# A fifth weight tile in the last group, 48 of 64 output groups turned while units run, and the first four weight slots freed one after another

## The chip, the cores and the metric

The kernel runs on all 8 cores of one Trainium2 chip. Each core takes 2048 of the 16,384 tokens and computes its whole result; the cores exchange nothing. The metric is the device time of the slowest core in microseconds (us). The two dies hold cores 0 to 3 and 4 to 7.

## The reference, cut to what matters

```python
# x: 4 x 4096 tokens of 4096 features
wb  = weight blocks (32 x 32), zeroed where the mask's block sums to 0
x1  = layernorm(x + x @ wb.T + bias)                    # layer 1
p   = softmax(x1 @ Wr.T); top 2 of 8 experts, renormed  # router
h   = einsum('ti,eri->ter', x1, A)                      # low rank, 8 x 16
lora = einsum('ter,te,eor->to', h, w, Bm) * 2
out = layernorm(x1 + x1 @ Wb.T + bias + lora)           # layer 2
```

Both layer norms run over the 4096 features of a token and have no gain or offset.

## The kernel before, in words

**Layout.** Activations lie transposed: features on the 128 partitions, tokens along the free axis. A core's 2048 tokens are four chunks (`tc` 0 to 3) of 512, its 4096 features 32 row tiles (`KT` = 32). `X` holds all of it in bf16. A weight tile (`n`, 32 for each layer) is 128 output features by 4096 inputs, 1 MB in bf16, cast by the DMA from 2 MB of f32; it lies in one of four slots `wt[0..3]` (tile number modulo 4).

**Units.** One unit is one weight tile by one chunk: 32 matmuls of 128x512 into one bank, and in layer 2 a 33rd for the low-rank part (`lora`, L484). `make_units` writes the order of all 260 units by hand, and every engine's program walks the same list, so `no` (1 to 260) is at once the unit's number and the value that semaphores `s_unit`, `s_evict`, `s_s1`, `s_s2` reach with it. Phase 0 is layer 1 (128 units), phase 1 layer 2 for chunks 0 and 1 (64 units), phase 2 layer 2 for chunks 2 and 3. VectorE evicts each unit (L660, L664: add the bias and the residual), ScalarE squares it (L928), VectorE adds both to the running sums `S1` and `S2` (L675, L682).

**The head.** The first 16 units (`HEAD`) take tiles 0 to 3 together, a chunk at a time: for each of eight pieces of X (four row tiles, one DMA of 1 MB f32 that becomes 512 KB, L305) all four tiles do four matmuls (L533 to L550). So units 13 to 16 end within a piece of each other. Tile 4 may be loaded into slot 0 once unit 13 is done (`LAST_OF_TILE`, L296). Phase 0's tiles need more: GpSimd loads the tile's mask in two halves into `ovA` (L290), VectorE sums its blocks (`sum_mask`, L620) and multiplies the weights (`clear_weights`, L635), which sets `s_wm`; TensorE waits for it. In the order of VectorE's program the sum of mask 4 comes after the eviction of unit 12, and the clearing of tile 4 after that of unit 14. All loads of masks, weights and X go through GpSimd's one queue, in program order. SyncE issues five small constants at the very start (L353 to L357), then the transposed residuals of phase 0 (`xres`, in `ovB`, L380).

**The tail.** Outputs of chunks 0 and 1 leave in the transposed layout through `ostg` (in `ovA`) and the host turns them; those 64 stores are over long before the end (the last is issued at 1735.5 us). Chunks 2 and 3 are turned on the core. The last four tiles (28 to 31, `GRP` = 4) run first for all of chunk 2, then for the first 256 tokens of chunk 3 (`FIRST_HALF`), then for its second 256 (`SECOND_HALF`), with 256-column matmuls. Sums per token come from `part_sums` in three parts (1024 tokens' first 512, next 256, last 256), each followed by `part_moments` on VectorE and `part_deviation` on ScalarE. There are 64 groups (128 tokens by 512 features): a `turn` is four matmuls against the identity (L528) into one of three side banks, `finish` scales the bank into an f32 stage in a dead part of `X` (L797 on VectorE for odd groups, L896 on ScalarE for even ones), and SyncE stores 256 KB (L413). `PART_AT` and `TURN_AT` say at which unit and after which matmul of it a part or a turn is issued. Groups 0 to 31 (chunk 2) are turned in units 254 to 260, up to five a unit; groups 32 to 63 after the last unit, when the four `pm` banks are free too (`tall`). A turn waits for the finish of the group three (then seven) before it, which has its bank.

Of the kernel before, what the change touches and what calls it, by code (L numbers as in the profile page):

```python
# [18 lines left out]
KT = D // 128  # L19
# [9 lines left out]
NW = 4  # L29
WT = KT + 1  # L30
# [3 lines left out]
NSQ = 2  # L34
NO = 4
GRP = 4


def make_units():

    u = [(0, n, tc) for tc in range(4) for n in range(GRP)]
    u += [(0, n, tc) for n in range(GRP, KT - GRP) for tc in range(4)]
    u += [(0, n, tc) for tc in (0, 1) for n in range(KT - GRP, KT)]
    u += [(0, n, tc) for n in range(KT - GRP, KT) for tc in (2, 3)]
    u += [(1, n, tc) for tc in (0, 1) for n in range(GRP)]
    u += [(1, n, tc) for n in range(GRP, KT) for tc in (0, 1)]
    u += [(2, n, tc) for n in range(KT - GRP) for tc in (2, 3)]
    u += [(2, n, tc) for tc in (2, 3, 3) for n in range(KT - GRP, KT)]  # L50
    return u


# [23 lines left out]
L2A_END = 192  # L77
NUNITS = len(UNITS)
HALF = TW // 2
FIRST_HALF = range(252, 256)  # L80
SECOND_HALF = range(256, 260)


def span(i):
# [21 lines left out]
def tile_no(ph, n):  # L106
    return ph * KT + n


LAST_OF_TILE = {}  # L110
# [4 lines left out]
def build_program():  # L115
# [28 lines left out]
    with contextlib.ExitStack() as st:  # L144
# [15 lines left out]
        g_t = ovB[:, 0:2048]  # L160
        wx = ovB[:, 2048:2560]
        wnx = ovB[:, 2560:3072]
        stg = [sbuf(f"stg{i}", [128, TW], BF16) for i in range(NST)]
        S1 = sbuf("S1", [128, T], F32)
        S2 = sbuf("S2", [128, T], F32)
# [64 lines left out]
        s_w = [sem(f"s_w{i}") for i in range(NW)]  # L230
# [53 lines left out]
        def _(g):  # L284
# [134 lines left out]
        def _(t):  # L419
# [59 lines left out]
            def lora(i):  # L479

                ph, n, tc = UNITS[i]
                w = wt[tile_no(ph, n) % NW]
                sp = span(i)
                t.matmul(pm[i % NB][:, 0:sp.stop - sp.start],  # L484
                         w[:, KT * 128:(KT + 1) * 128],
                         g_t[:, tc * TW + sp.start:tc * TW + sp.stop],
                         start=False, stop=True).then_inc(s_unit, 1)

            def part_sums(j):

                last = (252, 256, 260)[j]
                t.wait_ge(s_s1, last)
                t.wait_ge(s_s2, last)
                lo, hi = PARTS[j]
                for b in range(lo, hi):
                    o = 2 * TW + b * 128
                    t.matmul(plog[:, b:b + 1], S1[:, o:o + 128], onesf[:, 0:1],
                             start=True, stop=True)
                    mm = t.matmul(plog[:, 8 + b:9 + b], S2[:, o:o + 128],
                                  onesf[:, 0:1], start=True, stop=True)  # L500
                mm.then_inc(s_st, 1)

            def turn(g):

                b, q_ = g // 8, g % 8
                if g < 3:
                    if g == 0:
                        t.wait_ge(s_fin, 64)
                        t.wait_ge(s_evict, 252)
                    last = None  # L510
                elif g < 32:
                    last = g - 3
                elif g < 35:
                    last = (30, 31, 29)[g - 32]
                elif g < 39:
                    t.wait_ge(s_evict, 257 + g - 35)
                    last = None
                else:
                    last = g - 7
                if g == 32:  # L520
                    t.wait_ge(s_evict, 256)
                if g == 48:
                    t.wait_ge(s_evict, 260)
                if last is not None:
                    t.wait_ge((s_fa, s_fv)[last % 2], last // 2 + 1)
                o = (b % 4) * 128
                for j in range(4):
                    mm = t.matmul(tbank(g)[:, j * 128:(j + 1) * 128],  # L528
                                  xt(b // 4, 4 * q_ + j)[:, o:o + 128],
                                  ident[:, :], start=True, stop=True)  # L530
                mm.then_inc(s_tr, 1)


            for tc in range(NTC):
                for p in range(8):
                    t.wait_ge(s_x[tc][p], 16)
                    for n in range(GRP):
                        i = tc * GRP + n
                        if p == 0:
                            t.wait_ge(s_wm, n + 1)  # L540
                            if bank_user(i):
                                t.wait_ge(s_evict, bank_user(i))
                        for kt in range(4 * p, 4 * p + 4):
                            mm = t.matmul(  # L544
                                bank_of(i)[:, :],
                                wt[n][:, kt * 128:(kt + 1) * 128],
                                xt(tc, kt), start=(kt == 0),
                                stop=(kt == KT - 1))
                        if p == 7:
                            mm.then_inc(s_unit, 1)  # L550

            routed = None
            for i, (ph, n, tc) in enumerate(UNITS):
                if i < HEAD:
                    continue
                slot = tile_no(ph, n) % NW
                w = wt[slot]
                if ph == 1 and n == 0:
                    low_rank(tc)
                    routed = (tc, i)  # L560
# [3 lines left out]
                if ph == 0:  # L564
                    t.wait_ge(s_wm, n + 1)
                else:
                    t.wait_ge(s_w[slot], 16 * (tile_no(ph, n) // NW + 1))
                t.wait_ge(s_evict, bank_user(i))
                bank = bank_of(i)
                for kt in range(KT):  # L570
                    sp = span(i)
                    mm = t.matmul(bank[:, 0:sp.stop - sp.start],  # L572
                                  w[:, kt * 128:(kt + 1) * 128],
                                  xt(tc, kt)[:, sp], start=(kt == 0),
                                  stop=(ph == 0 and kt == KT - 1))
                    if routed and i == routed[1] and kt == 16:
# [19 lines left out]
                else:  # L596
                    if (ph, n) == (2, 0):
                        t.wait_ge(s_g, tc + 1)
                    lora(i)
            for g in range(32, 37):  # L600
                turn(g)
            part_sums(2)
            for g in range(37, GROUPS):
                turn(g)

        @block.vector
        def _(v):
# [191 lines left out]
                                ).then_inc(s_fv, 1)  # L799

            v.memset(wrt[:, KT * E:KT * E + 24], 0.0).then_inc(s_zero, 1)
            v.wait_ge(s_const[0], 16)
            v.wait_ge(s_const[1], 16)
            fin = 0
            for i, (ph, n, tc) in enumerate(UNITS):
                no = i + 1
                if i == 0:
                    for j in range(GRP):
                        sum_mask(j)
                        clear_weights(j)  # L810

                if ph == 1 and n == 0 and tc == 0:
                    normalise(1, 7)
# [38 lines left out]
                if no == 260:  # L852
                    finish(33)
            part_moments(2)
            for g in range(35, GROUPS, 2):
                finish(g)

        @block.scalar
        def _(sc):
# [48 lines left out]
            for i, (ph, n, tc) in enumerate(UNITS):  # L908
# [7 lines left out]
                if no == 254:  # L916
                    part_deviation(0)
                if no == 258:
                    part_deviation(1)
# [13 lines left out]
                if no == 260:  # L933
                    finish(32)
                    finish(34)
# [4 lines left out]
            for g in range(36, GROUPS, 2):  # L940
                finish(g)

    return nc
# [41 lines left out]
```

## Time and profile before

| | us |
|---|---|
| median of 3 runs | 1977.57 (1976.06 to 2238.74) |
| the profiled execution, device time | 1977.69 |
| its span, slowest core (core 6) | 1976.1 |
| spans of the 8 cores | 1971.2 to 1976.1 |

TensorE does its first matmuls at 36.45 us and runs for good from 69.00 on, when the last of the first four tiles is cleared; VectorE's first eviction starts at 94.24. From there on TensorE stands still at few places, which the rows below show.

All rows below are of core 6. Times in them are us from the start of its span. PE is TensorE's matmuls, DVE VectorE, ACT ScalarE, POOL GpSimd, SPq SyncE's issues of DMAs. A row of a timeline gives start, length, engine, line, operation, the names it writes and reads, and in brackets how long its engine had been idle and what released it.

### The profile page before, as it was taken

To read this page: it belongs to the slowest core of one execution; us is meant where nothing else is said; L and a number is where in the kernel's file an instruction comes from. 1 tells how busy PE (TensorE), PEld (TensorE's weight loads), DVE (VectorE), ACT (ScalarE), POOL (GpSimd) and SP (SyncE) were. 2 spreads that over 40 slices of the span, in tenths; PEclk is the share of its full clock that TensorE was granted. 3 is DMA by queue.
4 is the path that set the end of the run, shared out by engine and by line. 5 is a ranking of instruction groups with operands and counts; after the bars stand their busy time and mean duration, and the time that the engine had idled before them with its cause. 6 is when DMAs were issued, how large, how long until landed. Compare 5 with 4: busy or idle time off the path is not lost.

```text
span 1976.1 us, 25804 instructions; the slowest of 8 cores (1971.2 to 1976.1 us)
## 1 busy us (share of the span) xinstructions
PE 1875.1 (95%) x9068; PEld 870.8 (44%) x9068; DVE 1005.0 (51%) x1342; ACT 205.4 (10%) x331; POOL 146.2 (7%) x234
## 2 busy tenths in 40 slices
PE   0697999999999999999999999999999999999994
PEld 0243444444444444444444444444444444444464
DVE  3224555545555455667755876323325666633344
ACT  0001000010000001001111110001001010000023
POOL 1300000000000000003211000000000000000000
PEclk9798999999999999999999999999999999999997
DMA  9999988889888998999848455444556878844438
GB/s 156 175 190 155 138 114 106 112 121 124 109 106 115 123 121 107 126 165 205 171 125 145 87 97 95 80 82 85 94 104 135 182 170 183 191 91 80 77 101 252
DMA packets 125551, 256.72 MB, mean 130 GB/s; under 512 B 18544, under 2 KB 84336, under 8 KB 113008
## 3 DMA queue, kind: packets, MB, share of 16 engines
q0 software_dynamic: 27936, 154.22, 49.0%
q1 hardware_dynamic: 69840, 75.68, 21.6%
q10 hardware_dynamic: 27648, 25.18, 4.1%
q8 instruction: 73, 1.20, 0.2%
q14 instruction: 54, 0.44, 0.1%
HBM read 333.71 MB, written 58.72 MB: 199 GB/s over the span
## 4 chain that ended last, share of the span: by engine, by line
PE 94%; DMA 3%; DVE 1%; issue 0%; DVEq 0%; ACT 0%; POOL 0%; ACTq 0%; POOLq 0%
PE pm L572 83%; PE pm L544 3%; DMA ovA<-mask 2%; PE ph L448 1%; PE pm L484 1%; DMA wt<-w 1%; PE ph L544 1%; PE pstB L544 1%; PE plog L544 1%; PE pstA L544 1%; PE plog L454 0%; DVE bs L620 0%; PE pstA L432 0%; PE pstB L434 0%; DVE X L709 0%
## 5 line engine op out<-in xcount | busy, mean ns | idle before, releaser
L572 PE MATMUL pm<-X,wt 128*128 128x512 bf16 (+1 forms) x7808 | 1689.6, 376 | 11.5 <-DVE wt L635 11.5
L572 PEld LDWEIGHTS pm<-X,wt 128*128 128x128 bf16 x7808 | 761.9, 98 | 909.2 <-issue 20.9
L660 DVE SCALAR_TENSOR_TENSOR stg<-pm,bat,ovB 128x512 bf16<-128x512 f32 x120 | 90.1, 751 | 337.2 <-PE pm L572 272.9
L928 ACT ACTIVATE sq<-stg 128x512 f32<-128x512 bf16 x192 | 121.0, 630 | 1257.5 <-DVE stg L660 880.8
L682 DVE TENSOR_TENSOR S<-S,sq 128x512 f32<-128x512 f32 (+1 forms) x234 | 159.9, 683 | 23.4 <-issue 3.1
L620 DVE TENSOR_REDUCE bs<-ovA 128x2 f32<-128x2048 bf16 x64 | 143.7, 2279 | 32.5 <-DMA ovA<-mask 32.5
L664 DVE SCALAR_TENSOR_TENSOR X<-pm,bft,X 128x512 bf16<-128x512 f32 (+1 forms) x68 | 48.9, 719 | 184.8 <-PE pm L484 184.1
L664 DVE SCALAR_TENSOR_TENSOR stg<-pm,bft,X 128x512 bf16<-128x512 f32 x64 | 47.9, 750 | 172.9 <-PE pm L484 165.3
L675 DVE TENSOR_TENSOR S<-S,stg 128x512 f32<-128x512 f32 x168 | 116.3, 692 | 29.7 <-DVE stg L660 19.4
L544 PE MATMUL pm<-X,wt 128*128 128x512 bf16 x256 | 60.9, 402 | 63.6 <-DMA X<-xk 36.5
L301 POOL DMA_DIRECT2D wt<-wb x64 | 34.3, 536 | 807.8 <-PE pm L484 778.2
L290 POOL DMA_DIRECT2D ovA<-mask x64 | 34.5, 546 | 681.2 <-DVE bs L620 680.4
L709 DVE TENSOR_TENSOR X<-tmp,pstA 128x1024 bf16<-128x1024 f32 x64 | 78.2, 1221 | 7.0 <-DVE tmp L705 0.5
L928 ACT ACTIVATE sq<-X 128x512 f32<-128x512 bf16 (+1 forms) x68 | 41.1, 605 | 385.3 <-DVE X L664 385.3
L705 DVE TENSOR_TENSOR tmp<-X,pstB 128x1024 f32<-128x1024 bf16 x64 | 77.9, 1217 | 4.2 <-DVE X L709 1.9
L544 PEld LDWEIGHTS pm<-X,wt 128*128 128x128 bf16 x256 | 25.8, 102 | 98.0 <-issue 70.8
L635 DVE TENSOR_SCALAR wt<-wt,q 128x1024 bf16<-128x1024 bf16 x128 | 53.7, 483 | 23.2 <-DMA wt<-w 23.2
L675 DVE TENSOR_TENSOR S<-S,X 128x512 f32<-128x512 f32 (+1 forms) x66 | 43.6, 660 | 12.5 <-DVE X L664 12.5
L484 PE MATMUL pm<-ovB,wt 128*128 128x512 bf16 (+1 forms) x132 | 48.9, 373 | 0.0
L769 DVE TENSOR_TENSOR ovA<-ovA,pstA 128x512 f32<-128x512 f32 x64 | 44.1, 688 | 7.0 <-DVE ovA L768 0.5
L768 DVE TENSOR_TENSOR ovA<-stg,pstB 128x512 f32<-128x512 bf16 x64 | 43.6, 681 | 0.0
L333 POOL TENSOR_TENSOR S<-S,stg 128x512 f32<-128x512 f32 x18 | 20.8, 1154 | 116.3 <-DVE stg L660 74.3
(89 smaller groups left out, 413.1 us busy)
## 6 DMA issues: line engine op xcount, KB each, us to landing
wt<-wb POOLq DMA_DIRECT2D x64, 1056.0 KB, 9.6
ovA<-mask POOLq DMA_DIRECT2D x64, 512.0 KB, 8.6
wt<-w POOLq DMA_DIRECT2D x32, 1024.0 KB, 15.1
X<-xk POOLq DMA_DIRECT2D x32, 512.0 KB, 50.8
ovB<-X SPq DMA_DIRECT2D x512, 32.0 KB, 7.6
rdr<-stg ACTq DMA_DIRECT2D x128, 128.0 KB, 9.1
X<-rdr SPq DMA_DIRECT2D x32, 512.0 KB, 10.3
out<-ovA SPq DMA_DIRECT2D x64, 256.0 KB, 5.4
```

The source lines that it names most:

```text
L484: t.matmul(pm[i % NB][:, 0:sp.stop - sp.start], w[:, KT * 128:(KT + 1) * 128], g_t[:, tc * TW + sp.start:tc * TW + sp.stop], start=False, ...
L544: mm = t.matmul(bank_of(i)[:, :], wt[n][:, kt * 128:(kt + 1) * 128], xt(tc, kt), start=(kt == 0), stop=(kt == KT - 1))
L572: mm = t.matmul(bank[:, 0:sp.stop - sp.start], w[:, kt * 128:(kt + 1) * 128], xt(tc, kt)[:, sp], start=(kt == 0), stop=(ph == 0 and kt == ...
L620: v.tensor_reduce(bs[:, 2 * h:2 * h + 2].unsqueeze(2), mstg[h].rearrange("p (b e) -> p b e", e=1024), AX, ALU.add).then_inc(s_mred, 1)
L635: mm = v.tensor_scalar(wsl, wsl, q[n % 2][:, b:b + 1], None, ALU.mult)
L660: v.scalar_tensor_tensor(dst, bank, bat[:, n:n + 1], xres[i % NXR], ALU.add, ALU.add).then_inc(s_evict, 1)
L664: v.scalar_tensor_tensor(dst, bank, bft[:, n:n + 1], xt(tc, n)[:, sp], ALU.add, ALU.add).then_inc(s_evict, 1)
L675: v.tensor_tensor(S1[:, sl], S1[:, sl], dst, ALU.add).then_inc(s_s1, 1)
L682: v.tensor_tensor(S2[:, sl], S2[:, sl], sqr, ALU.add).then_inc(s_s2, 1)
L705: step(v.tensor_tensor(ts, xs, pstB[:, :].unsqueeze(1).broadcast_to([128, 2, TW]), ALU.mult))
L709: v.tensor_tensor(xs, ts, pstA[:, :].unsqueeze(1).broadcast_to([128, 2, TW]), ALU.subtract).then_inc(s_x1, 1)
L928: sc.activation(sq[i % NSQ][:, 0:sp.stop - sp.start], src, AF.Square).then_inc(s_sq, 1)
```

## The change

Five edits. (1) The last group has five tiles, 27 to 31 (`LGRP`), so there are 261 units and five half units on either side. (2) The very last tile (31 of layer 2) goes into `ovA` (the mask's buffer, later the output stages') and its low-rank block into 128 columns of `ovB` behind the residuals, after all 64 stores of chunks 0 and 1. (3) 48 groups (`GIN`) are turned while units run, in units 253 to 261, up to six a unit; 16 remain after the last unit. (4) In the head, the last chunk runs tiles 0 and 1 together over all pieces, then tile 2, then tile 3. (5) SyncE issues its constants after the second tile is cleared, and VectorE waits for the two biases after clearing all four.

```diff
-    u += [(2, n, tc) for n in range(KT - GRP) for tc in (2, 3)]
-    u += [(2, n, tc) for tc in (2, 3, 3) for n in range(KT - GRP, KT)]
+    u += [(2, n, tc) for n in range(KT - LGRP) for tc in (2, 3)]
+    u += [(2, n, tc) for tc in (2, 3, 3) for n in range(KT - LGRP, KT)]
...
-FIRST_HALF = range(252, 256)
-SECOND_HALF = range(256, 260)
+FIRST_HALF = range(NUNITS - 2 * LGRP, NUNITS - LGRP)
+SECOND_HALF = range(NUNITS - LGRP, NUNITS)
...
+PART_END = (251, 256, 261)
+GIN = 48
-PART_AT = {254: (0, 0), 257: (24, 1)}
-TURN_AT = {254: ((16, 0), (24, 1), (31, 2))}
-for _u in range(255, 261):
-    _g = 3 + 5 * (_u - 255)
-    TURN_AT[_u] = tuple((3 + 6 * _k, _g + _k) for _k in range(5) if _g + _k < 32)
+PART_AT = {253: (0, 0), 257: (24, 1)}
+TURN_AT = {253: ((16, 0), (24, 1), (31, 2)),
+           254: tuple((3 + 6 * _k, 3 + _k) for _k in range(5))}
+for _u in range(255, 262):
+    _g = 8 + 6 * (_u - 255)
+    TURN_AT[_u] = tuple((2 + 5 * _k, _g + _k) for _k in range(6)
+                        if _g + _k < GIN)
...
+        def wblk(i, kt):
+            if i == LAST_TILE:
+                return lora5 if kt == KT else ovA[:, kt * 128:(kt + 1) * 128]
+            return wt[i % NW][:, kt * 128:(kt + 1) * 128]
...
-        tall = tside + pm
+        tall = tside + [pm[1], pm[2], pm[3], pm[0]]
         def tbank(g):
-            return tside[g % 3] if g < 32 else tall[(g - 32) % 7]
+            return tside[g % 3] if g < GIN else tall[(g - GIN) % 7]
...
             def load_w(ph, n):
                 i = tile_no(ph, n)
+                if i == LAST_TILE:
+                    for j in range(NO):
+                        g.wait_ge(s_out[j], 16 * 64 // NO)
+                    g.dma_start(ovA[:, :], wb[n, :, 0:KT * 128]
+                                ).then_inc(s_w[NW], 16)
+                    g.dma_start(lora5, wb[n, :, KT * 128:WT * 128]
+                                ).then_inc(s_w[NW], 16)
+                    return
...
         def _(sy):
+            sy.wait_ge(s_wm, 2)
             sy.dma_start(bat[:, :], ba).then_inc(s_const[0], 16)
...
             def turn(g):
+                last = g - 3
+                if g == 0:
+                    t.wait_ge(s_fin, 64)
+                    t.wait_ge(s_evict, PART_END[0])
+                if g == 32:
+                    t.wait_ge(s_evict, PART_END[1])
+                if g == 48:
+                    t.wait_ge(s_evict, PART_END[2])
...
             for tc in range(NTC):
-                for p in range(8):
-                    t.wait_ge(s_x[tc][p], 16)
-                    for n in range(GRP):
+                for part in (((0, 1, 2, 3),) if tc < 3 else ((0, 1), (2,), (3,))):
+                    for p in range(8):
+                        if 0 in part:
+                            t.wait_ge(s_x[tc][p], 16)
+                        for n in part:
...
-            for g in range(32, 37):
+            for g in range(GIN, GIN + 3):
                 turn(g)
             part_sums(2)
-            for g in range(37, GROUPS):
+            for g in range(GIN + 3, GROUPS):
                 turn(g)
...
             v.memset(wrt[:, KT * E:KT * E + 24], 0.0).then_inc(s_zero, 1)
-            v.wait_ge(s_const[0], 16)
-            v.wait_ge(s_const[1], 16)
...
                         clear_weights(j)
+                    v.wait_ge(s_const[0], 16)
+                    v.wait_ge(s_const[1], 16)
...
-                if no == 254:
+                if no == 253:
                     part_moments(0)
```

The finishes of groups 32 to 34 that stood beside unit 260 go, since those groups are now finished in their units like the others; after the last unit both engines go on from group 48.

## Rows read from the trace of the kernel before

**Rows 1.** Page, part 1: busy time, share of the span, instructions.

```profile
PE 1875.1 (95%) x9068; PEld 870.8 (44%) x9068; DVE 1005.0 (51%) x1342; ACT 205.4 (10%) x331; POOL 146.2 (7%) x234
```

**Rows 2.** Waits: who waited for whom, us in total, times, longest.

```profile
PE pm L544 <- DVE wt L635: 27.1, 2, 16.3
PE pm L572 <- DVE wt L635: 11.5, 1, 11.5
...
PE ph L528 <- ACT X L896: 1.3, 1, 1.3
```

**Rows 3.** Timeline, end of the head and first unit behind it.

```profile
151.74 1.03 PE L544 MATMUL ph<-X,wt 128*128 128x512 bf16 x4
...
170.60 2.29 DVE L620 TENSOR_REDUCE bs<-ovA 128x2 f32<-128x2048 bf16 x1 [0.54 <-DMA ovA<-mask]
...
177.48 0.53 POOL L298 DMA_DIRECT2D wt<-w  x1 [108.01 <-PE ph L544]
...
189.07 1.67 DVE L635 TENSOR_SCALAR wt<-wt,q 128x1024 bf16<-128x1024 bf16 x4 [6.96 <-DMA wt<-w]
...
191.00 34.34 PE L572 MATMUL pm<-X,wt 128*128 128x512 bf16 x145 [11.47 <-DVE wt L635]
...
201.34 0.75 DVE L660 SCALAR_TENSOR_TENSOR stg<-pm,bat,ovB 128x512 bf16<-128x512 f32 x1 [1.18 <-PE pm L572]
...
203.04 0.69 DVE L682 TENSOR_TENSOR S<-S,sq 128x512 f32<-128x512 f32 x1
```

**Rows 4.** Line L305, first and last of its last 29 loads: issue, landing.

```profile
L305 POOL DMA_DIRECT2D X<-xk x1: 547/547/547, 52.6 to 52.6; - x1
...
DMA to landing us min/median/max: 17.2/17.2/17.2
...
L305 POOL DMA_DIRECT2D X<-xk x2: 891/894/897, 66.8 to 67.3; - x2
...
DMA to landing us min/median/max: 93.2/94.9/96.7
```

**Rows 5.** Windows: length, busy us by engine, clock, DMA share, GB/s.

```profile
170.00:175.00 5.00, 5.00 (x25) 2.25 (x23) 2.51 (x3) 0.00 (x0) 0.00 (x0) 1.00 0.76 42
...
185.00:190.00 5.00, 0.00 (x0) 0.00 (x0) 0.93 (x3) 0.00 (x0) 0.00 (x0) 0.50 0.95 161
190.00:195.00 5.00, 4.00 (x10) 1.46 (x11) 4.43 (x8) 1.26 (x2) 0.00 (x0) 0.50 1.11 205
```

**Rows 6.** Windows: half units 253, 254, 256 and 258, one each.

```profile
1900.95:1904.55 3.60, 3.60 (x35) 3.23 (x33) 2.14 (x3) 0.63 (x1) 0.00 (x0) 1.00 0.00 0
1904.55:1910.52 5.97, 5.97 (x63) 5.61 (x61) 2.97 (x9) 1.60 (x4) 0.00 (x0) 1.00 0.04 16
...
1915.24:1919.96 4.72, 4.72 (x55) 4.34 (x53) 3.31 (x6) 2.14 (x4) 0.00 (x0) 1.00 0.95 284
...
1925.49:1931.69 6.20, 4.88 (x56) 4.28 (x54) 4.19 (x11) 2.50 (x6) 0.00 (x0) 1.00 0.66 180
```

**Rows 7.** Timeline of the tail.

```profile
1909.46 5.80 SPq L413 DMA_DIRECT2D outt<-X  x7
...
1929.12 0.78 ACT L896 ACTIVATE X<-ph,nmt,rt 128x512 f32<-128x512 f32 x1
...
1940.79 0.27 PE L484 MATMUL pm<-ovB,wt 128*128 128x256 bf16 x1
...
1945.60 1.45 ACT L896 ACTIVATE X<-pm,nmt,rt 128x512 f32<-128x512 f32 x2
...
1956.02 0.80 DVE L797 TENSOR_SCALAR X<-pm,rt,nmt 128x512 f32<-128x512 f32 x1
```

**Rows 8.** Line L413, first store's landing; window of the stores after all units.

```profile
DMA to landing us min/median/max: 2.5/2.5/2.5
...
1950.00:1970.00 20.00, 4.41 (x58) 3.80 (x56) 6.81 (x10) 5.55 (x8) 0.00 (x0) 0.67 1.08 306
```

**Rows 9.** DMA queues from 0 to 21 us: packets, MB, share of 16 engines.

```profile
q1 hardware_dynamic: 720, 0.14, 4.7%
```

More of the change, by code:

```diff
@@ L36 @@
 GRP = 4
+LGRP = 5
 def make_units():
@@ L96, with slot_of @@
 PARTS = ((0, 4), (4, 6), (6, 8))
+PART_END = (251, 256, 261)
 GROUPS = 64
-PART_AT = {254: (0, 0), 257: (24, 1)}
-TURN_AT = {254: ((16, 0), (24, 1), (31, 2))}
-for _u in range(255, 261):
-    _g = 3 + 5 * (_u - 255)
-    TURN_AT[_u] = tuple((3 + 6 * _k, _g + _k) for _k in range(5) if _g + _k < 32)
+GIN = 48
[6 more added lines that the diff above has]
+                        if _g + _k < GIN)
 def tile_no(ph, n):
     return ph * KT + n
+LAST_TILE = 3 * KT - 1
+def slot_of(i):
+    return NW if i == LAST_TILE else i % NW
 LAST_OF_TILE = {}
@@ L162, in build_program @@
         wnx = ovB[:, 2560:3072]
+        lora5 = ovB[:, 3072:3200]
         stg = [sbuf(f"stg{i}", [128, TW], BF16) for i in range(NST)]
@@ L229, in build_program @@
         s_r = [[sem(f"s_r{tc}_{p}") for p in range(8)] for tc in range(NTC)]
-        s_w = [sem(f"s_w{i}") for i in range(NW)]
+        s_w = [sem(f"s_w{i}") for i in range(NW + 1)]
         s_mask = [sem(f"s_mask{i}") for i in range(2)]
@@ L481, in lora @@
                 ph, n, tc = UNITS[i]
-                w = wt[tile_no(ph, n) % NW]
                 sp = span(i)
                 t.matmul(pm[i % NB][:, 0:sp.stop - sp.start],
-                         w[:, KT * 128:(KT + 1) * 128],
+                         wblk(tile_no(ph, n), KT),
                          g_t[:, tc * TW + sp.start:tc * TW + sp.stop],
@@ L489, in part_sums @@
             def part_sums(j):
-                last = (252, 256, 260)[j]
+                last = PART_END[j]
                 t.wait_ge(s_s1, last)
@@ L505, in turn @@
                 b, q_ = g // 8, g % 8
+                last = g - 3
[6 more added lines that the diff above has]
+                    t.wait_ge(s_evict, PART_END[2])
                 if g < 3:
-                    if g == 0:
-                        t.wait_ge(s_fin, 64)
-                        t.wait_ge(s_evict, 252)
                     last = None
[L511 to L516, printed above, removed]
+                elif GIN + 3 <= g < GIN + 7:
+                    t.wait_ge(s_evict, NUNITS - 3 + g - GIN - 3)
                     last = None
-                else:
+                elif g >= GIN + 7:
                     last = g - 7
[L520 to L523, printed above, removed]
                 if last is not None:
@@ L534, in _ @@
             for tc in range(NTC):
-                for p in range(8):
-                    t.wait_ge(s_x[tc][p], 16)
-                    for n in range(GRP):
[L538 to L550, printed above, removed]
+                for part in (((0, 1, 2, 3),) if tc < 3 else ((0, 1), (2,), (3,))):
[3 more added lines that the diff above has]
+                        for n in part:
+                            i = tc * GRP + n
+                            if p == 0:
+                                t.wait_ge(s_wm, n + 1)
+                                if bank_user(i):
+                                    t.wait_ge(s_evict, bank_user(i))
+                            for kt in range(4 * p, 4 * p + 4):
+                                mm = t.matmul(
+                                    bank_of(i)[:, :],
+                                    wt[n][:, kt * 128:(kt + 1) * 128],
+                                    xt(tc, kt), start=(kt == 0),
+                                    stop=(kt == KT - 1))
+                            if p == 7:
+                                mm.then_inc(s_unit, 1)
             routed = None
@@ L555, in _ @@
                     continue
-                slot = tile_no(ph, n) % NW
-                w = wt[slot]
                 if ph == 1 and n == 0:
@@ L566, in _ @@
                 else:
-                    t.wait_ge(s_w[slot], 16 * (tile_no(ph, n) // NW + 1))
+                    j = tile_no(ph, n)
+                    t.wait_ge(s_w[slot_of(j)],
+                              32 if j == LAST_TILE else 16 * (j // NW + 1))
                 t.wait_ge(s_evict, bank_user(i))
@@ L572, in _ @@
                     mm = t.matmul(bank[:, 0:sp.stop - sp.start],
-                                  w[:, kt * 128:(kt + 1) * 128],
+                                  wblk(tile_no(ph, n), kt),
                                   xt(tc, kt)[:, sp], start=(kt == 0),
@@ L851, in _ @@
                     fin += 2
-                if no == 260:
-                    finish(33)
             part_moments(2)
-            for g in range(35, GROUPS, 2):
+            for g in range(GIN + 1, GROUPS, 2):
                 finish(g)
@@ L915, in _ @@
                     deviation(STATS_AT.index(no))
-                if no == 254:
+                if no == 253:
                     part_deviation(0)
@@ L932, in _ @@
                                  ).then_inc(s_spill[i % NST], 16)
-                if no == 260:
-                    finish(32)
-                    finish(34)
                 if ph == 1:
@@ L939, in _ @@
             part_deviation(2)
-            for g in range(36, GROUPS, 2):
+            for g in range(GIN, GROUPS, 2):
                 finish(g)
```

## The prediction

> **What bounds the kernel now.** Page, part 1, first: TensorE is busy for 95% of the span [rows 1], and the matmuls before and after are the same in number of columns. So only time in which TensorE stands still, or in which the kernel runs on after it, can be won. The view of waits says where it stands still: 27.1 us in two waits while the first tiles are cleared, 11.5 us in one more wait for a cleared tile, 1.3 us for a finish in the tail [rows 2]. The timeline around the second [rows 3]: the head's last chunk starts at 151.74 and TensorE goes idle at 191.00 - 11.47 = 179.53, so 128 matmuls take 0.217 us each. GpSimd issues tile 4 at 177.48, when unit 13 has ended; VectorE starts to clear it when it has landed, at 189.07; TensorE goes on at 191.00. Next the windows: the granted clock is 0.50 (1.2 GHz) from 185 to 195, and only 10 matmuls are busy in 190 to 195 [rows 5]. The unit that starts at 191.00 is evicted 10.34 us later [rows 3]; 32 x 0.217 = 6.9 and some 0.3 to the eviction would be 7.2. The low clock behind the stall thus costs 3.1 us more.
>
> In the tail the last unit's last matmul starts at 1940.79, so the units end at 1940.9; the last finish starts at 1956.02 [rows 7], and the span ends at 1976.1: for its last 19 us the kernel only stores. From 1950 to 1970 the DMA engines are full (share 1.08) at 306 GB/s [rows 8], 262,144 bytes in 0.857 us. So stores set the end, and what counts is when they start and whether they ever run dry.
>
> **The head (edit 4).** It leaves the count of matmuls alone; tiles 0 and 1 now end after 64 of the 128 instead of at the end. Step one: the pass over tiles 0 and 1 spends 8 x 0.217 = 1.73 us on a piece and wants the eighth at 151.74 + 7 x 1.73 = 163.8. That piece lands at 67.3 + 96.7 = 164.0 [rows 4]. I charge 0.4 us; the first piece cannot be late, since all earlier ones land over 3 us apart. Step two: unit 13 ends near 165.2, and tile 4 is issued then instead of at 177.48. Step three: GpSimd's queue still holds the two halves of mask 4, the second of which is summed from 170.60 on [rows 3]. From the first to the last of 29 X loads, 69.8 to 164.0, the queue moved one every 94.2 / 28 = 3.36 us [rows 4]; a tile is two of those, 6.7 us. Tile 4 lands at 170.5 + 6.7 = 177.2. From 170 to 175 the queues moved only 42 GB/s [rows 5], so there is room. Step four, VectorE: the mask's sum ends at 172.9; then come the evictions of units 13 and 14 with their sums, 201.34 to 203.73 in the like case, 2.4 us each [rows 3], so it is free at 177.7 and the clearing takes 191.00 - 189.07 = 1.9 us: 179.6. TensorE ends the head at 179.9 and needs tile 4 then. It is almost a tie; I take 180.4 and no fall of the clock, as an idle time of 1.3 us in the tail left it at 1.00 [rows 2, 6]. **Gain 191.0 - 180.4 + 3.1 = 13.7 us.** Bounds: 14.6 (no wait at all) and 5 (below, rival A). Tile 5 and mask 5 are queued behind tile 4 and are now also issued some 8 us earlier or more; they are needed four units (28 us) later, and the cover is gone only if they come over 15 us later than I think. Evictions of units 15 and 16 wait behind the clearing, as before; the bank of unit 17 is free since unit 9.
>
> **The start (edit 5).** Five DMA issues of SyncE, 720 packets, took 4.7% of the engines in the first 21 us [rows 9], 1.0 us. They delayed the first mask by at most that. Now the same packets come after the second of four tiles is cleared, still ahead of TensorE's start for good at 69.0 us, which the loads set. What mask 0 gains is given back: 0 us, bounds a gain of 1 and a loss of 1. VectorE's two waits move behind the clearings; the first eviction, at 94.2, is 25 us later still. SyncE's residual loads wait for X anyway.
>
> **The fifth tile (edits 1, 2).** A half unit takes 3.60 us, 66 of its matmuls 7.20 against 33 full ones at 0.217, 7.16 [rows 6, 3]: under 0.1 us. Its tile is loaded last in GpSimd's queue, behind tile 30, whose slot is free after unit 246; it is needed four full units (28 us) later, and the stores that it waits for are long over. The load is two DMAs instead of one. Nothing waits behind them. Cost 0.
>
> **The turns (edit 3).** I rebuild the end on the old clock. The half units start one full unit earlier, 1900.95 - 7.1 = 1893.8. A turn costs (4.72 - 3.60) / 5 = 0.224 us of TensorE; the first part's sums 5.97 - 3.60 - 0.67 = 1.7, the second's half of that [rows 6]. In unit 258 the chain sums, moments, deviation lets ScalarE finish only from 1929.12, 3.6 us into the unit, to 1929.90, and the fourth turn waits for that bank 1.3 us [rows 2, 6, 7]. Now the fourth turn stands at matmul 17 instead of 21, 2.54 us into the unit against 4.4: 1.9 us. Units end at 1893.8 + 10 x 3.60 + 48 x 0.224 + 1.7 + 0.85 + 1.9 = 1945.0. The same sum for the kernel before gives 1940.8; it was 1940.9. **So TensorE ends 4 us later, and the stores begin 7.1 us earlier**, at 1902.3 [rows 7].
>
> Do 48 stores keep ahead? They arrive at six per 3.60 + 6 x 0.224 = 4.94 us, 0.82 us each, against 0.857 at the full pace [rows 8] and 0.92 at the 284 GB/s of unit 256 [rows 6]. I take 0.89. 1902.3 + 2.5 (a lone store's landing, [rows 8]) + 47 x 0.89 = 1946.6; the 48th is finished about 1945.5 and lands by 1949. Then part 2 opens: the first finish starts 1945.60 - 1940.9 = 4.7 us behind the units, ready at 5.4 [rows 7], so 1950.4, issued at 1950.7. The 16 finishes take 6 us on two engines, faster than they can be stored. The last lands at 1950.7 + 2.5 + 15 x 0.89 = 1966.5; with 0.2 for SyncE's last wait the end is 1966.7, where it was 1976.1. **Gain 9.4 us**; what is late next is this chain behind the last unit, with the queue dry for a microsecond or two before it. Bounds: 10.5 (pace 0.82) and 4 (rivals B and C).
>
> The page HBM Reference of the Trainium skill, section Specifications (TRN2), gives about 358 GB/s for each core when both cores of a pair stream. No row here shows that; the full stretch shows 306. By the page a store would be an estimated 0.73 us and the gain some 2.4 us more.
>
> **The sum.** 13.7 + 9.4 = 23.1 us off the profiled execution's 1977.69: 1954.6. Cores whose last piece of X comes later relative to their head may lose some tenths more: **1955 us**. The profiled execution stands 0.1 us above the median, so the same number holds for it. That is 1.1%; about 2% (39.6 us) is what a measurement of this kernel can tell from no change.
>
> **Rivals.**
>
> A. *Tile 4 is late all the same.* Alone it took 11.5 us from issue to landing (177.48 to 189.0) with the queue empty [rows 3]. If it needs that long behind the mask, from 172.9, it lands at 184.4 and TensorE goes on at 186.3: 6.4 us idle, part of the clock's loss stays. Gain 5: 1963. For: the 11.5 us. Against: X's 3.36 us for half as much [rows 4]. Chance 0.14. A rule of the Trainium skill speaks for this one: SBUF — State Buffer, section "SBUF: two separate sides", says that GpSimd cannot write its DMA descriptors while VectorE runs certain two-port operations, and VectorE is busy from 170.6 to 177.7. GpSimd's issue of tile 4 took 0.53 us [rows 3], and no row here shows one held up.
>
> B. *Six turns a unit are too many.* Each turn waits for a finish three turns back, and finishes queue on VectorE behind the eviction and its sums. At five there was one wait [rows 2]. If each of the seven fuller units stretches by 0.8 us, TensorE ends 5.6 us later and so does all behind it: 1960. For: VectorE was busy 3.31 of 4.72 us with two finishes [rows 6]; with three it is 4.1 of 4.94. Against: at three turns of slack, 2.3 us, a finish of 0.8 fits. Chance 0.12.
>
> C. *The stores are bound from first to last.* Above 0.98 us a store, the 64 are one row: 1902.3 + 2.5 + 63 x 1.05 = 1971 at 1.05, gain 5: 1959. Against: 306 and 284 GB/s. Chance 0.09.
>
> D. *Head or tail does nothing*, since TensorE's end or a wait that I don't see takes its place: 1964 to 1968. Chance 0.04.
>
> E. *Slower than before.* The three side banks decide: if a fuller unit waits so long at each unit's start, behind eviction and sums, that it stretches by over 23.1 / 7 = 3.3 us, all is lost. At 3.6 us it would be 1980. The only stretch seen is 1.3 us in one unit of seven [rows 2]. Chance 0.03, and most of it would be just slower, not by 2%.
>
> The forecast has 0.58. Its own range is 1951 to 1958. The whole range must take in A to C and the bounds: **1950 to 1967**. Faster by over 2% needs 1938, out of reach of every sum here: 0.02. Slower by over 2%: 0.03. Within: 0.95.
>
> **What would show each step.** Head: the wait for a cleared tile at about 180 is under 1 us instead of 11.5, the clock stays at 1.00 from 175 to 200, tile 4 is issued near 165 and lands near 177. Tail: the first store is issued 43 us before the units end instead of 31; there is one wait of about 1.9 us in unit 258 and none else; 17 to 18 us of stores behind the first finish of part 2, at a share near 1. The prediction is wrong if tile 4 lands after 180, if several turns wait, or if the last 16 stores need more than 15 us.

## The result, and the profile after

| | before | after |
|---|---|---|
| median, us | 1976.88 (1976.06 to 2238.74, 4 runs) | 1964.99 (1964.27 to 1965.47, 4 runs) |
| ratio after / before | | 0.9941, 95% interval 0.9921 to 0.9960 |
| profiled execution, device time | 1977.69 | 1965.07 |
| its span, slowest core | 1976.1 (core 6) | 1963.5 (core 5) |

Some executions, of the old kernel and of changed ones, take 6 to 20% longer, with a lower granted clock on the cores of one die; the one of 2238.74 us is of that size, and ratios and comparisons leave such runs out.

The change is worth 12 us, or 0.6%. The forecast was 1955, so the time lies inside the range, and about half of the expected gain did not come. Two stretches are compared on all eight cores: from the start to the first half unit, and from there to the end. The medians are worked out from the traces.

| median of the 8 cores, us | before | after | gain | forecast |
|---|---|---|---|---|
| start to the first half unit (before: less the 7.1 of the full unit that moved) | 1893.9 | 1887.6 | 6.3 | 13.7 |
| first half unit to the end (before: plus 7.1) | 80.7 | 72.9 | 7.8 | 9.4 |

The split is good to about 1.4 us only: each kernel was traced in one execution, and the two runs below that keep one half of the old kernel differ from it by that much in the same half (the tail alone reaches its first half unit at 1892.5 with the old head; the head alone takes 79.3, with the 7.1, over the old tail). On such medians the two gains add up to 14.1 us; the slowest core, which sets the time, gained 12.6 in the traces.

First the waits of TensorE on core 5 of the kernel after (columns as in rows 2). The wait for a cleared tile behind the head is 6.0 us where it was 11.5 [rows 2]; 7.7 also holds one of 1.67 us at 874.64, of a kind that one core of the trace before has too. The wait in the tail grew from 1.3 to 2.0.

```profile
PE pm L572 <- DVE wt L663: 29.6, 2, 18.5
PE pm L600 <- DVE wt L663: 7.7, 2, 6.0
PE pstB L553 <- ACT X L922: 2.0, 1, 2.0
...
PE ph L572 <- DMA X<-xk: 0.8, 1, 0.8
```

The timeline of the same stretch as in [rows 3], on core 5:

```profile
165.39 1.02 PE L572 MATMUL ph<-X,wt 128*128 128x512 bf16 x4 [0.83 <-DMA X<-xk]
...
166.96 0.53 POOL L326 DMA_DIRECT2D wt<-w  x1 [99.09 <-PE ph L572]
...
172.01 2.29 DVE L648 TENSOR_REDUCE bs<-ovA 128x2 f32<-128x2048 bf16 x1 [0.56 <-DMA ovA<-mask]
...
178.39 0.75 DVE L688 SCALAR_TENSOR_TENSOR stg<-ph,bat,ovB 128x512 bf16<-128x512 f32 x1 [3.82 <-DMA ovB<-X]
...
182.54 0.75 DVE L688 SCALAR_TENSOR_TENSOR stg<-plog,bat,ovB 128x512 bf16<-128x512 f32 x1 [2.03 <-DMA ovB<-X]
...
185.18 1.67 DVE L663 TENSOR_SCALAR wt<-wt,q 128x1024 bf16<-128x1024 bf16 x4
...
187.10 18.09 PE L600 MATMUL pm<-X,wt 128*128 128x512 bf16 x74 [6.00 <-DVE wt L663]
```

Read the brackets. The last row but one, the clearing, has none: tile 4 was there already (landed at 179.44), and VectorE came late. It came late because ahead of the evictions of units 13 and 14 (178.39, 182.54) it stood idle until a DMA into `ovB` had landed, the residual `xres` that SyncE loads. In the trace before, the same two evictions (core 6) waited for TensorE or for nothing; their residuals had landed at 171.4 and 173.9 (medians of the cores):

```profile
177.32 0.75 DVE L660 SCALAR_TENSOR_TENSOR stg<-ph,bat,ovB 128x512 bf16<-128x512 f32 x1 [4.16 <-PE ph L544]
...
179.40 0.75 DVE L660 SCALAR_TENSOR_TENSOR stg<-plog,bat,ovB 128x512 bf16<-128x512 f32 x1
```

What the DMA engines did meanwhile stands in the DMA view from 170 to 175, first of the kernel before (core 6), then of the one after (core 5). A row gives packets, MB and the time that the packets took, as a share of the 16 engines; q1 is the queue of SyncE's loads, q0 GpSimd's.

```profile
q1 hardware_dynamic: 302, 0.21, 76.1%
```
```profile
q0 software_dynamic: 95, 0.75, 100.1%
q1 hardware_dynamic: 62, 0.05, 3.7%
```

Before, the residuals' small packets held 76% of the engines' time while they moved 42 GB/s. With tile 4 loaded beside them, GpSimd's queue has all of it and SyncE's nearly none. (In the experiments below SyncE's share is 81.7% with the tail alone, whose head is the old one, and 6.3% with the head alone.)

The windows behind it, against [rows 5]: the clock still falls to 0.50, only for a shorter time.

```profile
180.00:185.00 5.00, 1.09 (x6) 0.29 (x3) 2.30 (x4) 0.63 (x1) 0.00 (x0) 0.93 1.06 203
185.00:190.00 5.00, 2.90 (x7) 1.02 (x8) 1.84 (x5) 0.00 (x0) 0.00 (x0) 0.50 1.02 197
190.00:195.00 5.00, 5.00 (x22) 2.19 (x21) 4.26 (x7) 1.26 (x2) 0.00 (x0) 0.89 0.65 67
```

The tail on core 5, against [rows 6, 7]. The first row is the last matmul of chunk 2, so the half units start at 1890.82; the last matmul of the last unit starts at 1942.17; the first finish of part 2 at 1947.46; the span ends at 1963.5.

```profile
1890.60 0.38 PE L512 MATMUL pm<-ovB 128*128 128x512 bf16 x1
...
1942.17 0.27 PE L512 MATMUL pm<-ovB 128*128 128x256 bf16 x1
...
1947.46 0.78 ACT L922 ACTIVATE X<-ph,nmt,rt 128x512 f32<-128x512 f32 x1 [0.42 <-DVE nmt L814]
```

Windows of core 5 (a unit with six turns; unit 258; from the units' end to the first store of part 2; the last stores):

```profile
1905.11:1910.05 4.94, 4.94 (x59) 4.57 (x57) 3.58 (x7) 2.64 (x4) 0.00 (x0) 1.00 0.91 309
1920.62:1927.79 7.17, 5.12 (x59) 4.51 (x58) 4.41 (x12) 3.05 (x6) 0.00 (x0) 1.00 0.54 169
1942.20:1948.30 6.10, 3.57 (x39) 2.94 (x36) 2.96 (x10) 1.66 (x5) 0.00 (x0) 0.77 0.34 126
1948.30:1963.50 15.20, 4.00 (x36) 3.76 (x36) 5.03 (x7) 4.62 (x7) 0.00 (x0) 0.61 0.85 277
```

A unit with six turns takes 4.94 us without a wait, unit 258 stands for 2.05. The queues run nearly dry (0.34) before part 2, and the last stores go at a share of 0.85, not near 1.

### The profile page after: what moved, and what is told of

It is laid out like the page before. It is cut to its first block, busy times and chain, and to the rows that moved or that the text cites. A ratio compares the mean times of both kernels' runs of the same rounds, so it can differ in the third digit from the quotient of the medians.

```text
span 1963.5 us, 25888 instructions; the slowest of 8 cores (1955.9 to 1963.5 us)
## 1 busy us (share of the span) xinstructions
PE 1875.3 (96%) x9101; PEld 875.4 (45%) x9101; DVE 1005.3 (51%) x1345; ACT 205.7 (10%) x332; POOL 146.5 (7%) x235
## 4 chain that ended last, share of the span: by engine, by line
PE 91%; DMA 5%; DVE 2%; issue 1%; another core or an unknown queue 1%; SPq 0%; ACT 0%; POOL 0%; DVEq 0%; POOLq 0%; ACTq 0%
PE pm L600 82%; PE pm L572 3%; DMA ovA<-mask 3%; DMA wt<-w 2%; PE ph L477 1%; PE pm L512 1%; DVE bs L648 1%; DMA ovB<-X 1%; PE plog L483 0%; PE pstB L572 0%; PE pstA L572 0%; PE ph L572 0%; PE plog L572 0%; PE pstA L461 0%
## 5 line engine op out<-in xcount | busy, mean ns | idle before, releaser
L692 DVE SCALAR_TENSOR_TENSOR stg<-pm,bft,X 128x512 bf16<-128x512 f32 x64 | 47.9, 750 | 172.9 <-PE pm L512 165.3
L703 DVE TENSOR_TENSOR S<-S,X 128x512 f32<-128x512 f32 (+1 forms) x67 | 43.7, 653 | 12.6 <-DVE X L692 12.6
## 6 DMA issues: line engine op xcount, KB each, us to landing
wt<-w POOLq DMA_DIRECT2D x32, 1024.0 KB, 15.6
X<-rdr SPq DMA_DIRECT2D x32, 512.0 KB, 10.3
```

What stands on the lines that cost most here:

```text
L692: v.scalar_tensor_tensor(dst, bank, bft[:, n:n + 1], xt(tc, n)[:, sp], ALU.add, ALU.add).then_inc(s_evict, 1)
L703: v.tensor_tensor(S1[:, sl], S1[:, sl], dst, ALU.add).then_inc(s_s1, 1)
```

## The experiments

Each ratio is to runs of the kernel before that were taken beside that run (medians 1975.8 to 1977.1), with a 95% interval. "Faster than before" is worked out from the ratio unless two times are given. A difference to the changed kernel is one of medians (1964.99 us) that were taken at different times; on differences under some 2 us it says little.

### The tail alone

```diff
-                for part in (((0, 1, 2, 3),) if tc < 3 else ((0, 1), (2,), (3,))):
+                for part in ((0, 1, 2, 3),):
...
-            sy.wait_ge(s_wm, 2)
```

(and VectorE's two waits for the biases back at the start)

> The changed kernel with the head's order and the place of the constants put back, so only the fifth tile and the 48 turned groups are left. If the two traces are read rightly, the head stalls 11.5 to 12.5 us again with the clock down behind it, and from the first half unit to the end the run is like that of the changed kernel: about 8 us faster than before (1969). The prediction's own term for it is 9.4 us (1967.5). A rival, that most of the 12 us came from the tail and the head gave nothing, wants 1965.

Measured: 1970.04 us, ratio 0.9965 (0.9953 to 0.9977), 6.9 us faster than before. TensorE waits for tile 4 again, 12.34 us on core 6. From the first half unit to the end the median core takes 72.8 us, the changed kernel 72.9. The first theory holds; the rival does not. And with the head's old order the residuals of units 13 and 14 land at 171.2 and 173.9 again, as before the change, not at 175.9 and 181.4: it is the head's new order that makes them late.

### The head alone

This edit is against the kernel before.

```diff
             for tc in range(NTC):
-                for p in range(8):
-                    t.wait_ge(s_x[tc][p], 16)
-                    for n in range(GRP):
+                for part in (((0, 1, 2, 3),) if tc < 3 else ((0, 1), (2,), (3,))):
+                    for p in range(8):
+                        if 0 in part:
+                            t.wait_ge(s_x[tc][p], 16)
+                        for n in part:
...
```

> The kernel before with nothing but the head's last chunk in the order tiles 0 and 1, tile 2, tile 3. Theory: VectorE clears tile 4 behind the evictions of units 13 and 14, and these wait for residuals that SyncE may load only when all of X has landed; so TensorE still stands 5 to 6 us and its clock still falls: 4 to 6 us faster than before (1972). Rival, the prediction's term: 13.7 us faster (1963). Rival, tile 4 lands late and is the only cause: the clearing starts within 0.3 us of its landing.

Measured: 1971.16 us, ratio 0.9974 (0.9963 to 0.9984), 5.1 us faster. With the tail's 6.9 this makes 12.0, what both together gave: within the intervals (some 2 us each way) the two halves add. The timeline of its core 0:

```profile
165.83 0.53 POOL L298 DMA_DIRECT2D wt<-w  x1 [96.60 <-PE ph L546]
...
182.14 0.75 DVE L662 SCALAR_TENSOR_TENSOR stg<-plog,bat,ovB 128x512 bf16<-128x512 f32 x1 [2.35 <-DMA ovB<-X]
...
184.78 1.67 DVE L637 TENSOR_SCALAR wt<-wt,q 128x1024 bf16<-128x1024 bf16 x4
...
186.71 3.57 PE L574 MATMUL pm<-X,wt 128*128 128x512 bf16 x8 [6.74 <-DVE wt L637]
```

The clearing again starts without an idle time before it, 5.8 us after tile 4 has landed (178.97), so the landing is not what holds it.

### Tile 4 cleared ahead of the two evictions

```diff
 CLEAR_AT = {4 * n - 2: n for n in range(GRP, KT - GRP)}
+del CLEAR_AT[14]
+CLEAR_AT[12] = 4
```

> The changed kernel, but VectorE clears tile 4 right after mask 4's sum, ahead of the evictions of units 13 and 14. If those evictions (their residuals) hold the clearing, TensorE's wait near 185 falls from 5 or 6 us to under 1.5 us, the clock stays up, and the whole is 7 to 9 us faster than the changed kernel (1957). If tile 4's own landing (about 179) is what counts, the wait falls by 3 us at most and the clock falls still: 3 us faster (1962). If the evictions that now come later hold the bank or the spill of a unit that follows, a new wait of some us stands behind unit 17.

Measured: 1957.50 us, ratio 0.9902 (0.9887 to 0.9916), 7.5 us less than the changed kernel. Core 5, the slowest:

```profile
178.88 1.67 DVE L665 TENSOR_SCALAR wt<-wt,q 128x1024 bf16<-128x1024 bf16 x4 [4.29 <-DMA wt<-w]
180.61 0.75 DVE L690 SCALAR_TENSOR_TENSOR stg<-ph,bat,ovB 128x512 bf16<-128x512 f32 x1
180.81 11.38 PE L602 MATMUL pm<-X,wt 128*128 128x512 bf16 x52 [0.36 <-DVE wt L665]
```

Its windows from 175 to 190 (as in rows 5):

```profile
175.00:185.00 10.00, 9.63 (x46) 4.23 (x44) 4.97 (x10) 1.26 (x2) 0.91 (x2) 1.00 1.04 185
185.00:190.00 5.00, 5.00 (x25) 2.26 (x24) 2.35 (x4) 0.63 (x1) 0.00 (x0) 1.00 1.01 214
```

Now the clearing waits for tile 4's landing, TensorE for 0.36 us, and the clock stays at 1.00. The median core reaches the first half unit at 1880.2, a head gain of 13.7 us against 1893.9: the forecast's number, to be had once VectorE's order is right. No new wait stands behind unit 17. This shows what cost the head its gain: the place of the clearing behind two evictions that wait for residuals.

### Mask 5 and tile 5 held back

```diff
                     k = 2 * n + h
+                    if k == 10:
+                        g.wait_ge(s_evict, 14)
```

> The changed kernel, but GpSimd issues mask 5 (and tile 5 behind it) only after unit 14 is evicted. It tells what makes the residuals of units 13 and 14 land at 178 and 182 instead of 171 and 174. Theory A: mask 5 and tile 5, issued from 172 and 175 on, take the engines' time: then unit 14's residual lands near 177, the wait at 187 shrinks by 4 us and the whole is 4 to 6 us faster than the changed kernel. Theory B: it is tile 4 itself, in the queue from 167 on: then the residuals land within 1.5 us of where they did, and the time is the same or slower, since tile 5 comes later.

Measured: 1961.93 and 1962.13 us, two runs, ratio 0.9925 (0.9906 to 0.9944), 3 us less than the changed kernel. The median core reaches the first half unit at 1884.9 instead of 1887.6. Medians over the cores of when residuals have landed:

| residual of unit | before | after | mask 5 held |
|---|---|---|---|
| 13 | 171.4 | 175.9 | 175.9 |
| 14 | 173.9 | 181.4 | 178.9 |
| 15 | 176.7 | 186.7 | 179.6 |

Neither theory is right alone. Of unit 14's 7.5 us, 2.5 go with mask 5 and tile 5 away, and of unit 15's 10.0, 7.1; the 4.6 of unit 13 and most of unit 14's rest stay, with tile 4 and the halves of mask 4 beside them. Mask 4 was loaded then in the kernel before too, so what is left is tile 4; from 170 to 175 GpSimd's queue has 97.9% of the engines on core 4 of this run too. In line L409's view of the kernel after (issues from 165.3 to 167.9, and from 167.9 to 171.0) the loads take 7.6 and 9.2 us in the median, and up to 11.5; in that of the kernel before (nearly the same loads, issues from 164.1 to 165.9, and from 165.9 to 168.7), 4.9 and 4.3:

```profile
DMA to landing us min/median/max: 4.0/7.6/10.4
DMA to landing us min/median/max: 7.4/9.2/11.5
```
```profile
DMA to landing us min/median/max: 4.8/4.9/5.4
DMA to landing us min/median/max: 4.0/4.3/5.4
```

### Part 1's moments behind two finishes

```diff
+MOM_G = 29
...
-                if no == 258:
-                    part_moments(1)
                 for _kt, g in TURN_AT.get(no, ()):
                     if g % 2:
                         finish(g)
+                    if g == MOM_G:
+                        part_moments(1)
```

(on ScalarE the same with `part_deviation(1)`)

> The changed kernel, but the moments and the deviation of part 1 come after the finishes of groups 28 and 29 in unit 258, not before those of 26 and 27. Theory: the fourth turn of unit 258 waits 2.05 us for ScalarE's finish of group 26, which stands behind the deviation for no need, and on some cores that wait takes the clock down for a while (53.0 us from the first half unit to the end of the units instead of 51.3). Then the wait goes, all cores take 49.3 us, and the kernel is 2 to 3 us faster than the changed one. Rival: the stores are bound by bandwidth alone, so TensorE's earlier end moves nothing: within 0.5 us of it.

Measured: 1964.41 us, ratio 0.9936 (0.9923 to 0.9949), 0.6 us less than the changed kernel, which can't be told from nothing. The traces say more. The wait of 2.05 us is gone; three short ones remain on the slowest core:

```profile
PE ph L554 <- ACT X L923: 2.5, 2, 2.1
...
PE pstB L554 <- ACT X L923: 0.3, 1, 0.3
```

(2.1 of the 2.5 lie behind the last unit.) From the first half unit to the units' end every core takes 50.2 us, not the 49.3 I gave, where the changed kernel's take 51.3 on five cores and 53.0 on three. From there to the end it is 21.8 instead of 21.3: a part of TensorE's gain waits for the stores. The median core gains 0.9 us from the first half unit on, and its head happened to be 1.0 us later. So my theory is right on the wait, too high on its worth. The time alone does not refute the rival; what speaks against it is the stretch from the first half unit to the end, 72.0 us here and 71.8 in the run with both edits, against 72.9 in the changed kernel and 73.2 with the tile cleared first.

What the wait does to the clock can be seen within one kernel, the changed one. First core 2, then core 5, windows around the wait in unit 258:

```profile
1918.00:1922.00 4.00, 2.23 (x26) 1.80 (x23) 2.58 (x10) 1.47 (x4) 0.00 (x0) 1.00 0.35 109
1922.00:1926.00 4.00, 3.73 (x28) 3.08 (x29) 1.77 (x3) 1.57 (x3) 0.00 (x0) 0.64 0.76 271
```
```profile
1924.00:1928.00 4.00, 2.40 (x28) 2.27 (x29) 2.08 (x4) 2.52 (x5) 0.00 (x0) 1.00 0.45 157
1928.00:1932.00 4.00, 4.00 (x49) 3.69 (x47) 3.28 (x6) 2.07 (x4) 0.00 (x0) 1.00 0.88 313
```

Both cores stood for the same 2.05 us. On core 2 the clock fell behind it (0.64 on the mean of 4 us, between 1.2 and 2.4 GHz) and the unit cost 1.65 us more; on core 5 it did not. It fell on 2 to 7 of 8 cores in each of the six kernels that have this wait, and on none of the 16 cores of the kernel before and of the head alone, whose wait there is 1.3 us. In the three kernels traced without the wait it fell on none of 24 cores. The length of the wait alone does not decide: waits of 2.98, 2.47, 2.34 and 2.14 us for X's last piece (head alone, core 3; tile cleared first, core 4; both edits with the constants at the start, core 5; eight stores left out, core 5) left it at 1.00, one of 2.05 (mask 5 held back, core 5) did not. What does decide stays open.

### Both edits

The cleared tile's two lines and the moments' edit in one kernel.

> The changed kernel with both edits: tile 4 cleared ahead of the evictions of units 13 and 14, and part 1's moments behind the finishes of groups 28 and 29. The two runs apart gave 7.5 and 0.6 us. If they touch different stretches they add: 1956.5 to 1957, some 20 us faster than the kernel before.

Measured: 1954.68 us, ratio 0.9888 (0.9872 to 0.9904), 10.3 us less than the changed kernel and 22 less than before. This is the forecast's 1955, by the forecast's head and a tail without the wait. It is 2 us under what I expected of a plain sum: on top of the cleared tile the moments gave 2.8 us, not 0.6. A reason that fits, argued and not shown: with the tile alone three cores had lost the clock in unit 258, the slowest among them, and none does here; the median core gained 1.4 from the first half unit on.

### The constants at the start again

```diff
-            sy.wait_ge(s_wm, 2)
...
             v.memset(wrt[:, KT * E:KT * E + 24], 0.0).then_inc(s_zero, 1)
+            v.wait_ge(s_const[0], 16)
+            v.wait_ge(s_const[1], 16)
```

> The changed kernel with the constants issued at the very start again and VectorE's two waits before the first clearing. The prediction's term for it is 0, within 1 us either way (1964 to 1966): mask 0 lands 1 to 2 us later, but TensorE's start near 69 us does not move. Rival: the early masks are on the path, then it is over 1 us slower.

Measured: 1964.19 us, ratio 0.9935 (0.9921 to 0.9949), 0.8 us less than the changed kernel. In the median of the eight cores mask 0 is summed from 8.3 us on with the change, from 9.7 before and from 9.4 here, and TensorE starts for good at 69.3, 68.9 and 68.5: what was gained at first is given back. No run shows that the edit is worth anything, and its sign stays open.

With this put back and both edits from above together:

> The kernel with both edits (clearing first, moments later), and the constants issued at the very start again. The run with that alone was 0.8 us faster than the changed kernel, which its own spread does not separate from nothing. If the constants cost something where they are now, this is 0.5 to 1 us under the 1954.7 of the two edits; if the order does nothing, it is within 0.5 us of it either way.

Measured: 1954.07 us, ratio 0.9891 (0.9874 to 0.9907), 0.6 us less than with both edits, the lowest median of all. But its ratio is no lower (0.9891 against 0.9888), and the two intervals nearly coincide: no difference is shown.

### Eight stores left out

```diff
-            for g in range(GROUPS):
+            for g in range(GROUPS - 8):
```

(the last waits are set to match; the last eight groups of the output are missing)

> The changed kernel without the stores of the last eight groups (56 to 63), which are left out of the output. The tail is bound by stores if each of these costs its 0.8 us: 6 to 6.5 us faster (1958.5). If the finishes of VectorE and ScalarE were the bound it would move by under 3 us, since the last of them starts some 9 us before the end.

Measured: 1957.9 to 1959.4, ratio 0.9909 (0.9893 to 0.9925), 6 us less than the changed kernel, 0.7 to 0.8 us a store, where a bound by the finishes would have allowed under 3. The median core ends 15.6 us after its units instead of 21.3. The end is set by the stores.

## Why the prediction was right on the range and half wrong on the size

**What bounds the kernel.** Right. TensorE's waits and the stores behind the last unit were the two places, and the two halves of the change add up.

**The head, steps one to three.** Nearly right. X's last piece kept TensorE for 0.8 us on core 5 and 0 to 1.2 on the others (0.4 charged), tile 4 was issued at 166.96 and landed at 179.44 (I said 165.2 and 177.2; medians 166.1 and 178.9). The pace of 6.7 us a tile behind the mask came out at 7.5.

**The head, step four.** This is the step that failed, and with it 7.4 of the forecast's 13.7 us. It put the evictions of units 13 and 14 right behind the mask's sum, 2.4 us each, and had VectorE free at 177.7. The evictions wait for a third thing, the residuals on SyncE's queue. I had looked at that queue for the constants, and wrote that it waits for X anyway, but not what stands behind that wait: the residuals of units 13 to 16 may be loaded only when the last piece of X is there, at 164, and these units now end 11 us earlier while the loads are not issued earlier. That alone would have cost little: 171.4 and 173.9, when they landed before, is ahead of the end of the mask's work (174.57 on core 5), and two evictions of 2.4 us behind it would end at 179.4, when tile 4 lands (an estimate from these rows). The loss is in an overlap that the sum did not have: the tile that the change moves forward made the residuals land later, unit 13's at 175.9 and unit 14's at 181.4. A row that I had read said so: from 170 to 175 I took the 42 GB/s for room, but the share beside it in the same row was 0.76 [rows 5], and it was just these residuals that held the engines. VectorE was free at 185.2 instead of 177.7. Clearing the tile ahead of the evictions brought the 13.7 us; that it is the same number to the tenth is luck, since the head moves by 1.4 us from one execution to the next.

**The clock behind the stall.** The 3.1 us were right in size: from TensorE's restart to the first half unit the kernel before takes 1702.8 us on core 6 (1900.95 - 7.12 - 191.0), the one with the tile cleared first 1699.9 on core 5 (1880.74 - 180.81), 2.9 less; the other cores before, but for one with a wait of its own, give 2.1 to 2.7. Little of it was won: a stall of 3 to 6 us was also followed by a fall, and the same stretch takes 1701.4 to 1702.6 us on the seven cores after that have no other wait, so 1.5 to 2.7 are still lost.

**Rival A** had the time that the change would take if tile 4 were late (a gain of 5, 1963). Its number is near what happened in the head (6.3), but its mechanism did not happen: the tile was there 4 to 6 us before it was cleared. The rule of the Trainium skill that stood beside it (SBUF — State Buffer, section "SBUF: two separate sides", on GpSimd's descriptors while VectorE runs two-port operations) is not seen at work in this trace: the issue of tile 4 took 0.53 us again, and from issue to landing it took 12.2 us in the median core, where it took 12.1 before. A row that ends in the right number is no proof of the mechanism beside it.

**The start and the fifth tile.** No effect of either is seen, as said (0 us each); no wait for the tile in `ovA` shows in the tail.

**The turns.** Units' end 51.2 us behind the first half unit was forecast, 51.3 measured, the wait in unit 258 1.9 and 2.05; rival B and rival E are out, since no other turn waits. Missed was that this longer wait takes the clock down on some cores. The stores: 21.7 us from the units' end to the end forecast (1966.7 - 1945.0), 21.3 the median, 20.3 to 21.8 the range. On core 5 the first store of part 2 came 0.4 us later behind the units than I said (6.1), and the last 16 took 14.9 us from first issue to last landing where I had 15.9. (My own sign of being wrong, over 15 us for these 16, thus stood under my own forecast.) A store takes 0.84 us on core 5, (1963.24 - 1950.62) / 15, where I had 0.89. The absolute sum, 72.9 us from the first half unit on, is exact, in part because these small errors cancel; the gain of 9.4 was too high all the same, because it was taken against core 6, which before needed 35.4 us behind its units where the median core needed 33.7.

**Rival C** is out: the share of 0.34 before part 2 shows the queue dry. The Trainium skill's page HBM Reference, section Specifications (TRN2), gives 358 GB/s for a core. Over the last 15.2 us of stores it was 277, and 309 in a unit with six turns; but in the run without eight stores the first seven slices of the row below, 3.15 us, have 369 in the mean, above the page's number. The measured stretches decide: 0.73 us a store would have been too low.

```profile
GB/s 369 310 369 382 387 391 378 282 23 27 18 0 0 0 0 0 0 0 0 18 382 373 305 305 341 314 196 319 351 364 396 387 323 205 73 23 23 0 0 0
```

(This row is the DMA view of that run from 1940 to 1958, in 40 slices.)

## What to carry to other kernels

When work is moved earlier, list for each instruction that now comes early everything it waits for, also what was never waited for before: a load that used to be ready by 6 us can be the new bound. In an engine with one order, put the step that the critical engine waits for ahead of the steps that only somebody else needs; here that one line was worth more (7.5 us) than the reordering without it (5.1). When you ask whether the DMA engines have room for a load, read the share of their time, not the GB/s: small packets fill the one at a low figure of the other. And take the baseline of a sum from all cores, not from the slowest, whose excess may be in a stretch of its own.

## What the hardware showed that was not expected

An idle time of 2.05 us between dense matmuls was followed by a fall of TensorE's clock on some cores and by none on others, in one kernel and one execution, and cost 1.65 us where it came; 1.3 us in the tail never was, and 2.98 us at one place in the head was not either. Small loads from one part of the on-chip memory to another (32 KB, 4.3 to 4.9 us in the median) took 7.6 to 9.2 us once the load of a weight tile ran beside them: their queue's share of the engines' time from 170 to 175 went from 76.1% to 3.7%, while the tile's own landing was late by only 0.8 us over the pace of the X loads.
